# Products of the identity with itself in TensorE's gaps: 14 in the first two slots, 18 in the last one

## What is computed

```python
x = x + 0.5 * ffn0(layernorm(x))        # x @ int4(kernel) + bias + (x @ a) @ b
x = x + attn0(layernorm(x))             # retention, 8 heads of 16, group norm, silu gate, @ W_O
x = x + 0.5 * ffn0(layernorm(x))
x = x + 0.5 * routed(layernorm(x))      # router scores, top half of the tokens through gelu FFN 128-512-128
x = x + attn1(layernorm(x))             # chunked retention, 4 heads, keys of 32, values of 64, @ Wo
x = x + 0.5 * routed(layernorm(x))
```

## Time and profile before

| | us |
|---|---|
| median of three executions | 814.96 |
| lowest and highest of them | 813.86, 816.46 |
| the profiled execution | 813.06 |
| its span, first to last instruction | 811.1 |
| TensorE busy in it | 756.5 |
| VectorE busy | 666.2 |
| GpSimd busy | 475.4 |
| ScalarE busy | 424.5 |
| mean granted clock of TensorE, of 1 | 0.982 |

### The profile page before, as it was taken

The page is one execution under the profiler, slowest core; times in us unless marked ns, Lnnn a source line. Parts: engine busy times, 40 slices in busy tenths (PEclk is TensorE's granted clock), DMA queues, the critical chain, the costliest instruction groups (busy, mean ns, idle before and its releaser), DMA issues.

```text
span 811.1 us, 29578 instructions
## 1 busy us (share of the span) xinstructions
PE 756.5 (93%) x13001; PEld 612.8 (76%) x13001; DVE 666.2 (82%) x1825; ACT 424.5 (52%) x875; POOL 475.4 (59%) x375
## 2 busy tenths in 40 slices
PE   5768999999999999998789999999999999999785
PEld 4657788887888878776578888887888888888653
DVE  6687888888888999986748889987777988888777
ACT  2434555565655456564444446655544566554645
POOL 3578888888887788776333444444434344453434
PEclk9998999999999999999899999999999999999988
DMA  7000101100001000010000000000000000001113
GB/s 229 29 28 29 29 28 29 29 28 3 29 28 29 29 29 2 3 55 2 1 2 2 3 3 2 2 2 2 2 3 2 3 2 2 2 2 29 41 39 105
DMA packets 23285, 18.57 MB, mean 23 GB/s; under 512 B 2147, under 2 KB 20469, under 8 KB 22901
## 3 DMA queue, kind: packets, MB, share of 16 engines
q1 hardware_dynamic: 22596, 16.40, 6.7%
q10 hardware_dynamic: 560, 0.28, 0.1%
HBM read 12.48 MB, written 4.19 MB: 21 GB/s over the span
## 4 chain that ended last, share of the span: by engine, by line
PE 74%; DVE 17%; POOL 4%; ACT 3%; issue 2%; DMA 0%; DVEq 0%; POOLq 0%; ACTq 0%
PE ps L286 20%; PE ps L410 11%; PE ps L401 10%; PE ps L281 5%; PE ps L671 4%; PE ps L364 3%; PE ps L297 3%; PE ps L384 2%; PE ps L308 2%; PE ps L394 2%; DVE x L1221 2%; POOL grstd L1063 2%; PE ps L663 2%; PE ps L356 2%; PE ps L320 2%
## 5 line engine op out<-in xcount | busy, mean ns | idle before, releaser
L1063 POOL TENSOR_TENSOR grstd<-gve,mhalf 128x32 f32<-128x32 f32 (+1 forms) x32 | 159.0, 4968 | 26.8 <-DVE gve L1276 26.8
L410 PEld LDWEIGHTS ps<-w_s,hid 128*128 128x128 f32 x1024 | 125.4, 195 | 8.2 <-issue 7.2
L410 PE MATMUL ps<-w_s,hid 128*128 128x128 f32 x1024 | 130.3, 280 | 0.0
L401 PE MATMUL ps<-xt_r,w_s 128*128 128x512 f32 x256 | 126.6, 618 | 0.7 <-ACT xt_r L818 0.7
L822 ACT ACTIVATE hid<-ps,b_s 128x512 f32<-128x512 f32 x128 | 84.0, 725 | 25.8 <-PE ps L401 25.7
L1069 POOL TENSOR_TENSOR um<-um 128x96 f32<-128x96 f32 (+1 forms) x32 | 21.3, 665 | 90.6 <-DVE um L1255 90.6
L1059 POOL TENSOR_TENSOR r_ret<-ve_ret,powers 128x8 f32<-128x8 f32 x32 | 57.8, 1807 | 28.0 <-DVE ve_ret L1207 28.0
L401 PEld LDWEIGHTS ps<-xt_r,w_s 128*128 128x128 f32 x256 | 45.2, 191 | 36.1 <-issue 31.2
L1249 DVE TENSOR_TENSOR sc<-ps,tri 128x1024 f32<-128x1024 f32 (+1 forms) x64 | 58.3, 953 | 16.7 <-PE ps L320 10.0
L286 PE MATMUL ps<-w_qkvg,xt_p 128*128 128x128 f32 x512 | 69.4, 280 | 2.8 <-ACT xt_p L818 2.8
L1054 POOL TENSOR_TENSOR rstd_ln_mod<-ve_ln_mod,mhalf 128x4 f32<-128x4 f32 x32 | 32.3, 1010 | 65.9 <-DVE ve_ln_mod L1207 65.9
(11 more groups left out here) (236 smaller groups left out, 1748.5 us busy)
## 6 DMA issues: line engine op xcount, KB each, us to landing
xtin<-in_xt SPq DMA_DIRECT2D x16, 256.0 KB, 3.6
out_x<-base SPq DMA_DIRECT2D x16, 256.0 KB, 2.3
xin<-in_x SPq DMA_DIRECT2D x15, 256.0 KB, 3.0
rot<-in_rot SPq DMA_DIRECT2D x2, 1024.0 KB, 5.9
w_s<-in_w SPq DMA_DIRECT2D x2, 256.0 KB
xin<-in_x ACTq DMA_DIRECT2D x1, 256.0 KB, 4.0
w_qkvg<-in_wqkvg SPq DMA_DIRECT2D x1, 256.0 KB, 3.8
w_qkv<-in_wqkv SPq DMA_DIRECT2D x1, 256.0 KB
```

Source lines behind the costliest of these rows:

```text
L401: nc.tensor.matmul(bank(k), w1_s[:, f, :], xt["r"][:].rearrange("p j n -> p (j n)"), start=True, stop=True).then_inc(s[f"h{f}"], 1)
L410: mm = nc.tensor.matmul(bank(k, j * P, P), hid[:, f, j * P:(j + 1) * P], w2_s[:, f, :], start=False, stop=(f == last and j == NT - 1), ski ...
L1063: nc.gpsimd.tensor_tensor(grstd[:, 0:n], gve[:, 0:n], mhalf[:, 0:n], ALU.pow) \
```

## The change

A helper `keep_busy(times, k)` in TensorE's program multiplies the identity by itself into the first 128 columns of bank k, `times` times. Nothing reads the results, no semaphore is raised by them, and each bank is written anew by its next user. It is called in seven places: twice 2 in the prologue, 2 ahead of `centre_first` and 5 ahead of the wait for the rotated keys in slot -1, 3 at the start of slot 0, and 18 in `slot_end` behind `transpose_y`: 32 products, 64 matmul records. Nothing else changes.

```diff
+            def keep_busy(times, k):
+                for _ in range(times):
+                    nc.tensor.matmul(bank(k, 0, P), ident, ident, start=True, stop=True)
+
             pe.wait_ge(s["w_lead_in"], 16)
+            keep_busy(2, 7)
             pe.wait_ge(s["w_step"], 2)
             nc.tensor.transpose(bank(0, 0, P), peaks, ident).then_inc(s["w_pe"], 1)
...
             nc.tensor.matmul(bank(2, 0, P), half_r[:], bias_r[:], start=True, stop=True).then_inc(s["w_pe"], 1)
+            keep_busy(2, 7)
             pe.wait_ge(s["w_step"], W_KERNEL)
...
                 if finish:
                     routed_down(0, AT["mod"], last, 0, 2)
+                if g == 0:
+                    keep_busy(3, 2)
                 if sl.prepare:
                     wait(pe, f"xt_in{sl.buf(1)}", sl.landed(1))
...
                 if g < 0:
+                    keep_busy(2, 5)
                     centre_first()
...
                     routed_up(2, up[2])
+                if g < 0:
+                    keep_busy(5, 2)
                 if sl.prepare and not route:
                     wait(pe, "qkr", new)
                     wait(pe, "v", new)
...
                 transpose_y(now)
+                keep_busy(18, X1)
                 wait(pe, "ln_mod_xn", old)
                 wait(pe, "ystore", sl.count(-2))
                 transpose4("ln_mod", h, X2)
```

## The result

The changed kernel takes 811.83 us (median of 8 executions, 809.62 to 812.48) against 814.63 for the kernel before (8 executions, 813.13 to 816.82). The ratio is 0.9953 with a 95% interval of 0.9938 to 0.9967; measured once more, it was 0.9940 (0.9927 to 0.9953). The prediction said 812.8, a gain of 2.2, which it took to be most likely too small to be told from none.

The account below looks back on a forecast made before the run. TensorE, busy for 93% of the span, sets the pace by the order of its own work, except at clock dips. Terms -2.0 + 0.5 - 0.5 = -2.0, taken as -2.2 with an allowance: 814.96 becomes 812.8 us, range 811.0 to 815.3.

Parts of the forecast that it names:

- The end: Last slot, 18 products behind the transposes of y: full clock held, end 1.96 us earlier, term -2.0, bounds -0.9 and -2.3.
- The cover: Last slot: the 18 products take 4.28 us inside TensorE's idle 4.96, leave some 0.66 and cost nothing.
- the rank rounds: Last slot: VectorE's chain alternating with small TensorE products is late next; its L447 product can run 1.96 us earlier.
- The prologue: Six products before the first slots, run at the low clock level: term +0.5 us, bounded by 0 and +1.0.
- The bound of 0, that denser work lifts the clock earlier: Prologue: lower bound of the +0.5 us term, no delay if denser work lifts the clock earlier.
- The stream of instructions: Inserted instructions move stalls such as L364's 0.76 us of "issue"; one may go, another come: 0, bounded by -0.8 and +0.8.
- The slots: Slots -1 and 0, 5 and 3 products in idle gaps: no clock fall at 21.7 us, term -0.5, bounds 0 and -1.7.
- Rival 1: Start weighs more: slot 0 usually runs slower than profiled, products there save 1.7 us; -3.5, 811.5 us, chance 0.18.
- a change within 0.3%: Whole kernel: a change under about 2.4 us, not told from none; chance 0.52, against faster 0.41 and slower 0.07.
- The dips in slot 2 and at the change-over: Low clock at 64 us and in the twentieth slice: the diff adds nothing near either, so both stay.
- Rivals 2 and 3: The products don't hold the clock, 815.5 us, chance 0.10; or those of the last slot run slowly, 817.4 us, chance 0.06.
- Rival 4: Only the end counts, at its lower bound of -0.9, and the start little: -0.5, 814.5 us, chance 0.16.

## Why the prediction was right or wrong

**The end: right.** The cover held (4.18 us against 4.28 predicted, 0.92 left against 0.66), the transposes of the gated y came to wait for VectorE, and the rank rounds were what was late next. The term was -2.0; the trace shows -2.31 and the run with the end alone -2.0 with an interval of -3.1 to -1.0. The 0.3 beyond it in the trace come from a later round, whose product no longer stands so long behind the output product.

**The prologue: right, but hidden.** The first two products delay the transpose of the peaks: 4.33 against 3.75, of which 0.24 are the lead DMA's, which landed later by that much in this execution, and 0.34 theirs. The second two cost nothing, as said: L432 is behind by the same 0.58. The third two and the late rise take the products with `w_qkvg` to +1.33, or +1.1 without the DMA's part, a little over my upper bound of 1.0; over all traces the mean is the +0.5 of the sum. Alone, though, the six came out at 0.9992 (0.9981 to 1.0002), in which the predicted +0.5 us (1.0006) no longer lies; the trace of that kernel shows both stalls gone, which more than pays for the delay. The bound of 0, that denser work lifts the clock earlier, isn't shown: of the four traces with these products the centring of the weights still ran slowly in two (1.91 and 1.92 us).

**The stream of instructions: the step that failed.** I saw the 0.76 us of "issue" in L364, on the chain, and wrote "0, bounded by -0.8 and +0.8". The runs show about -1.0 there, and another -0.8 at L394, which the prediction didn't look at: in all ten traces with products in the first slots or the prologue both are gone, in all four without they are there. With the estimate of -1.8 in its place the sum is -2.0 + 0.5 - 0.5 - 1.8 = -3.8 us, beside the -3.8 and -4.9 of the two ratios. The parts fit as well: the slots alone would be -0.5 - 1.8 = -2.3 (measured -2.2), the start -1.8 (-2.0), and the prologue alone -1.3 (-0.7, with an interval down to -1.5). That these stalls go with instructions inserted ahead is shown; why they do is open.

**The slots: the clock's part right for the profiled execution.** The 0.47 us at the scores are the predicted -0.5. What I took too lightly is that other executions fall longer. The profiled one was the fastest of the four that I had, and of the four traces with this start one shows a fall of 6.8 us instead of 3.4. I did write that the timed runs lay 0.8 to 3.4 us above the profiled one, and then allowed 0.2 for it. Rival 1, which read this spread as longer falls in slot 0, said -3.5 and so came near the measured size, in good part by luck: most of what it put down to the clock is the stalls. The page "TensorE: Matmul & The Clock Gate" of the Trainium skill, in the section that the prediction cites, says that the number of slow matmuls differs from run to run. The runs agree that the low time does, with 25.9 to 40.8 us at the low level for one and the same program.

**The chances.** I held a change within 0.3% most likely, and the two measurements are beyond it. The forecast stood 0.2 us short of that line, and the missing 1.8 us of the stalls carry it across. The dips in slot 2 and at the change-over stayed as predicted, but the first can be twice as long as in the profile of before. Rivals 2 and 3 fell: the clock held, and the products started at the full level. Rival 4 fell too, since the end alone gave 2.0 and not 0.9.

## What to carry to other kernels

A profile is one draw: if a fall of TensorE's clock lies behind a gap, compare the profiled execution's time with the timed ones before sizing it, and take the mean clock of every execution, not the one trace. An idle time put down to "issue" on the chain is a term of the sum when instructions are inserted ahead of it, and one trace can't say which way it goes: look for it in the first trace after the change. Products in a gap paid here when they really streamed data and ended before the operand came. Two single places paid by themselves, the end with 2.0 us and the first slots with 2.2, much of the latter by the stalls; in slot 1 and at the change-over a single filling only moved the fall to the next idle stretch, and filling these too took 4.3 us off the changed kernel.

## What the runs showed of the hardware

36 records with one column each kept TensorE as "busy" as 36 with 128 (4.08 and 4.18 us), and the clock fell all the same. One and the same program spent between 25.9 and 40.8 us at 1.2 GHz, by the execution. What a low stretch costs depends on where it lies: in two kernels alike but for the 9 products in slot 1, 6.8 us of it in slot 2 went with 2.0 us more of time where it ended at 73.0 us than where it ended at 67.3. And two stalls without a releaser, of 0.41 to 0.76 and of 0.53 to 0.55 us, were there in all four traces with nothing inserted ahead of them and in none of the ten with 12 or more records inserted ahead.
